# Unread products at the start of a scan, another order of the last weight loads, and row weights turned by a small product, in a state space block with a routed mixture of experts

## The reference

```python
xc = conv(in_proj_w @ ctx); u = silu(xc + conv_b)
dt_lo, Bm, Cm = split(x_proj_w @ u)
delta = softplus(dt_proj_w @ dt_lo + dt_proj_b)
# over the 256 positions, for each channel and each of 16 states:
state = state * exp(delta * A) + (delta * u) * B ; y = sum_n(state * C)
x = x + tanh(g_xattn) * (y + D * u) * silu(layernorm(x))
t = layernorm(x)
logits = t @ gate_w ; top 2 of 8 ; top_w = softmax(top two logits)
x = x + tanh(g_ffn) * sum_e top_w[e] * ((silu(t @ w0[e]) * (t @ w1[e])) @ wo[e])
```

## Time and profile before

| | |
|---|---|
| three runs | 294.03, 294.96, 295.08 us; median 294.96 |
| the profiled execution | 295.31 us, its span 293.1 us |
| busy share of the span | PE 89%, DVE 79%, ACT 63%, POOL 60% |
| mean granted clock of TensorE | 0.975 of full |
| chain that ended last | PE 60%, DVE 15%, issue 11%, POOL 6% |

### The profile page before, as it was taken

One profiled execution on the slowest core, in us unless ns is written; L12 is line 12 of the kernel. 1 busy time (PEld: TensorE's weight loads), 2 busy tenths in 40 slices (PEclk: granted clock), 3 DMA queues, 4 the chain that ended last, 5 costly groups with the idle time before them and its releaser, 6 DMA issues.

```text
span 293.1 us, 4667 instructions
## 1 busy us (share of the span) xinstructions
PE 261.4 (89%) x1177; PEld 177.8 (61%) x1178; DVE 231.1 (79%) x403; ACT 184.9 (63%) x343; POOL 175.1 (60%) x159
## 2 busy tenths in 40 slices
PE   7985597899888998888997999999999999999970
PEld 7432242344344354433476877989898989898960
DVE  2989979999999998999979649888565666566640
ACT  2895747865775657788895326565757575757540
POOL 6103168898999898989810331546564746464342
PEclk9999789999999999999999979999999999999996
DMA  7699400000000001000099310333333333333212
GB/s 237 201 390 386 178 2 0 1 0 0 0 1 2 1 0 72 0 0 3 0 330 356 122 54 22 47 61 46 63 48 62 48 62 48 59 50 57 32 25 36
DMA packets 16677, 22.73 MB, mean 78 GB/s; under 512 B 2570, under 2 KB 10290, under 8 KB 16658
## 3 DMA queue, kind: packets, MB, share of 16 engines
q1 hardware_dynamic: 11472, 16.41, 16.1%
q0 software_dynamic: 4416, 6.03, 12.6%
q10 hardware_dynamic: 770, 0.06, 0.2%
HBM read 17.38 MB, written 5.11 MB: 77 GB/s over the span
## 4 chain that ended last, share of the span: by engine, by line
PE 60%; DVE 15%; issue 11%; POOL 6%; ACT 3%; DMA 2%; POOLq 1%; DVEq 0%; ACTq 0%
PE PD L1062 11%; PE PZ L1102 11%; PE PU L1062 10%; PE PY L862 8%; DVE states L1270 5%; POOL hC L422 4%; PE PY L1088 4%; DVE states L1276 4%; PE PY L857 2%; PE PZ L1053 2%; PE PU L770 1%; PE PD L807 1%; PE PU L841 1%; DMA x_rows<-u 1%; PE PZ L903 1%
## 5 line engine op out<-in xcount | busy, mean ns | idle before, releaser
L422 POOL TENSOR_TENSOR hC<-states,WO 128x512 f32<-128x512 f32 x63 | 79.8, 1280 | 16.8 <-PE PY L862 11.7
L1276 DVE TENSOR_TENSOR_SCAN states<-PD,states 128x512 f32<-128x512 f32 x64 | 77.4, 1211 | 1.1 <-ACT PD L632 0.9
L862 PE MATMUL PY<-hC,ident 128*128 128x512 f32 x128 | 68.1, 616 | 4.1 <-POOL hC L422 3.8
L457 POOL DMA_INDIRECT out<-lg,y_at x23 | 37.0, 1607 | 48.3 <-ACT lg L736 41.1
L632 ACT ACTIVATE PD<-WO,Aneg 128x510 f32<-128x510 f32 x64 | 43.8, 688 | 16.9 <-DVE states L1276 13.7
L1270 DVE TENSOR_TENSOR states<-PU,WO 128x512 f32<-128x512 f32 x64 | 42.7, 669 | 2.6 <-POOL hC L422 1.3
L443 POOL DMA_INDIRECT hC<-x_rows,x_at x23 | 27.2, 1183 | 28.4 <-DMA x_rows<-u 17.3
L720 ACT ACTIVATE hidT_hi<-PY 128x512 fp32r<-128x512 f32 x23 | 13.8, 599 | 38.8 <-PE PY L1088 38.8
L1521 DVE TENSOR_TENSOR WO_lo<-WO,WO_hi 128x512 fp32r<-128x512 f32 x46 | 29.7, 687 | 6.1 <-issue 5.7
L862 PEld LDWEIGHTS PY<-hC,ident 128*128 128x128 f32 x128 | 22.7, 192 | 17.4 <-POOL hC L422 11.0
L1509 DVE TENSOR_TENSOR dA<-PU,dA 128x512 f32<-128x512 f32 x23 | 15.9, 690 | 21.1 <-PE PU L1062 21.1
(11 more groups left out here) (242 smaller groups left out, 505.6 us busy)
## 6 DMA issues: line engine op xcount, KB each, us to landing
W<-in_L_ffn_w SPq DMA_DIRECT2D x16, 512.0 KB, 10.5
WO<-in_L_ffn_wo SPq DMA_DIRECT2D x8, 512.0 KB, 6.4
xs<-in_x SPq DMA_DIRECT2D x2, 512.0 KB, 5.6
out<-xs SPq DMA_DIRECT2D x2, 512.0 KB, 4.9
early<-in_ctx SPq DMA_DIRECT2D x1, 512.0 KB, 4.3
x_rows<-u SPq DMA_DIRECT2D x1, 512.0 KB, 3.3
x_rows<-u SPq DMA_DIRECT2D x2, 256.0 KB, 3.1
hC<-x_rows,x_at POOLq DMA_INDIRECT x23, 3.2
```

Source lines behind the costliest of these rows:

```text
L422: pool.tensor_tensor(hC[:, n % 2, :], states[:, n % RING, :], C_rep[:, pair % C_RING, :], ALU.mult).then_inc(hc_done, 1)
L457: pool.indirect_dma_start(out=out, out_offset=bass.IndirectOffsetOnAxis(ap=y_at[:, s:s + 1], axis=0), in_=y_tile[s % 2], in_offset=None, c ...
L862: pe.matmul(PY[:, h, :], ident[:, :], hC[:, n % 2, :], start=False, stop=(m == DS - 1)).then_inc(y_done, 1)
L1276: dve.tensor_tensor_scan(states[:, n % RING, :], DEC[n % 2], states[:, n % RING, :], 0.0, ALU.mult, ALU.add).then_inc(scan_done, 1)
```

## The change

1. **Unread products at the scan's start.** Two products of the identity by `u`, 128x512, are put before `spread_B(0)` (into the bank that it then fills) and two before `spread_C(1)` (into bank 5). Nobody reads them.
2. **Rows and loads.** `normed` of the first 512 rows leaves tiles 59 to 62 and stands on ACT behind the last gates of the scan, ahead of the table load. SP loads wo of experts 0 to 3 first, then stores the three parts of `x_rows` and the second half of x2, and loads wo of experts 4 to 7 last. Each pair of experts has a semaphore of its own, and ACT waits for a pair only at the first slot that can use it.
3. **Row weights.** In the second run of one-hot products the operands are exchanged, so that the result lies as 48 x 128 (`W_ROWS`); ACT copies it, and one small product with a doubled identity (`two_id`, made by POOL at the start) turns it back and adds the two parts. DVE copies once where it copied and added. The layout of `slot_w` is changed to suit.
4. **Fills.** "placed" 8 to 4, "rows" (three times 1) gone, "weights" 6 to 7, "turned" 4 (new, behind the row weights); "turn" stays 3. `xT_out(0, 0)` on ACT moves ahead of `WO_out(0, 0)`.

```diff
-NORMED_AT = (59, 60, 61, 62)
...
-FILL = {"placing": 10, "placed": 8, "rows": 1, "weights": 6, "table": 1, "turn": 3}
+FILL = {"placing": 10, "placed": 4, "weights": 7, "table": 1, "turned": 4, "turn": 3}
...
+        W_ROWS = bank[4][0:2 * COLS, 0:P]
...
             store_x2(0)
             sp.wait_ge(dbu_done, NT)
             sp.wait_ge(exp_done, NT)
-            store_rows(0)
             load_WO(0)
             load_WO(1)
+            store_rows(0)
+            store_x2(1)
+            store_pair(2)
+            store_pair(3)
+            sp.wait_ge(x2_ps, NQ * QB)
+            load_WO(2)
             sp.wait_ge(hc_done, NT - 1)
             sp.wait_ge(last_hc, 1)
             load_WO(3)
-            sp.wait_ge(x2_ps, NQ * QB)
-            load_WO(2)
-            store_x2(1)
-            store_pair(2)
-            store_pair(3)
...
-                    if n in NORMED_AT:
-                        normed((NORMED_AT.index(n),))
...
             base_out(1)
+            normed(range(QBLK))
             act.preload_act_table_set("natural_log_exp_and_others")
...
-            act.wait_ge(ld["wo"], 16 * E)
...
+            act.wait_ge(w_rows_ps, 1)
+            act.activation(w_rows[:, :], W_ROWS, ACT.Copy).then_inc(w_rows_ok, 1)
+            xT_out(0, 0)
             act.wait_ge(slots_ok, 1)
+            act.wait_ge(WO_in[0], 32)
             WO_out(0, 0)
-            xT_out(0, 0)
             xT_out(1, 1)
...
             for s in range(4):
+                if s % 2:
+                    act.wait_ge(WO_in[(s + 1) // 2], 32)
                 expert_tile(s, s % 2, 16 * ((s - 1) // 2) if s > 2 else None)
+            act.wait_ge(WO_in[3], 32)
...
+            pe.wait_ge(taps_ok[1, 0], DC - 1)
+            for _ in range(2):
+                pe.matmul(BCR[0], ident[:, :], u[:, 0, 0, :], start=True, stop=True)
             pe.wait_ge(sel_ok, 1)
             pe.wait_ge(consts, 7)
             spread_B(0)
...
             x_dbl(1)
+            for _ in range(2):
+                pe.matmul(PY[:, 1, :], ident[:, :], u[:, 0, 0, :], start=True, stop=True)
             spread_C(1)
...
             for j in range(n):
                 if j % 4 == 0:
-                    if j:
-                        fill("rows", PD[1][:, :])
                     pe.wait_ge(row_hot_ok, j // 4 + 1)
...
-                mm = pe.matmul(bank[5][:, 0:2 * COLS].rearrange("p (i s) -> p i s", i=2), row_hot[:, j, :], slot_w[:, :, j, :], start=(j == 0), stop=(j == n - 1))
-            mm.then_inc(w_at_ps, 1)
+                mm = pe.matmul(W_ROWS, slot_w[:, j, :, :].rearrange("p i s -> p (i s)"), row_hot[:, j, :], start=(j == 0), stop=(j == n - 1))
+            mm.then_inc(w_rows_ps, 1)
+            fill("turned", PD[1][:, :])
...
             x_turn(0, 0, 16)
+            pe.wait_ge(two_ok, 1)
+            pe.wait_ge(w_rows_ok, 1)
+            pe.matmul(bank[5][:, 0:COLS], w_rows[:, :], two_id[:, :], start=True, stop=True).then_inc(w_at_ps, 1)
             fill("turn", PD[1][:, :])
...
             dve.tensor_copy(w_at[:, :], bank[5][:, 0:COLS]).then_inc(w_at_ok, 1)
-            dve.wait_ge(w_at_ok, 1)
-            dve.tensor_tensor(w_at[:, :], w_at[:, :], bank[5][:, COLS:2 * COLS], ALU.add).then_inc(w_at_ok, 1)
```

25 lines of the change are left out of this document (15 added, 10 removed).

## The result

| | before | after |
|---|---|---|
| median of four runs | 294.54 us | 297.28 us (296.14 to 298.51) |
| profiled execution | 295.31 us, span 293.1 | 296.14 us, span 294.2 |
| granted clock in it | 0.975 | 0.989 |

A forecast was written before the change was run, and what follows sets the result against it. The scan was taken as DVE-bound with POOL close behind, then latencies, then PE's products. Terms summed to -2.97 us, 0.3 was given back: 292.6 for the profiled execution, 292.3 against the median, range 291.2 to 294.8.

The forecast's parts named there:

- Scan, -2.05: Scan's start: unread products keep PE's clock up, so DVE's three idle stretches go, saving 2.05 us.
- rival 1: Scan's start: the clock still falls, only later; DVE keeps some 1.3 of 2.05 us, 293.6 us; chance 0.18.
- Norms, +0.5: Behind the scan: the moved norms delay ACT's copy; DVE waits and everything behind is late by 0.5 us.
- table and row weights: Between scan and slot 0: exchanged products and changed fills bring PE to the turn at the old time, 0 us.
- Rival 3: Table: one clock fall of some 3.4 us makes PE 0.7 to 1.4 late, about 293.3 us; chance 0.15.
- rival 4: Table to gate: the clock fall lasts 6.8 us, costing PE 4.5 us; slower, 296 to 297.5 us; chance 0.08.
- Gather, +0.4: First gather: shares the DMA engines in halves with the last loads, 0.4 us longer; ends 0 and +2.7.
- rival 2: First gathers: loads hold gather 0 for 1.5 to 2.7 us, delaying all slots, 293.4 to 294.6 us; chance 0.12.
- Store, -0.5: Last store: finds an empty queue instead of 4 MB of wo, saving 0.5 us; bounds 0 and -1.0.
- Second hole, -0.35 and -0.97: Just before and in slot 0: PE stays at 2.4 GHz, saving 0.35 us on fills and 0.97 on the gate.

The follow-up runs named there:

- e12: e3 with the norms of the first rows at their new place behind the scan: 296.91 us, ratio 1.012.
- e3: The changed kernel with part 2 undone (SP's old order, norms at tiles 59 to 62): 293.94 us, ratio 1.001.
- e11: The changed kernel with the loads of experts 4 to 7 held until gathers 0 to 3 have landed: 296.20 us, ratio 1.008.
- e2: The changed kernel with the loads of experts 4 to 7 held until gathers 0 and 1 have landed: 299.72 us, ratio 1.021.
- f5: e12 with the fills of the kernel before: 297.87 us, ratio 1.012.
- f6: e12 with fourteen "placing" fills instead of ten, ahead of PE's idle stretch: 294.65 us, ratio 1.003.
- e6: The changed kernel with only the loads of experts 6 and 7 held until gathers 0 to 3 have landed: 296.18 us, ratio 1.007.
- e10: Kernel before with parts 1 and 3, five more unread products, three fills behind the row weights, loads of experts 4 to 7 held for four gathers: 292.86 us.
- f1: e11 with the fills of the kernel before: 294.75 us, ratio 1.004.

## Why the prediction was wrong

**Scan, -2.05: right in the profile, wrong in the median.** All three idle stretches of DVE went and the scan ended 1.8 us earlier. But a profile is one execution. Over 12 runs part 1 alone brings 0.2 us, for two reasons. The clock falls near 34 us in part of the executions all the same (nine of 14 profiles), so rival 1 was a matter of how often, not whether. And the loss that was to be won back is not in every execution of the kernel before: two of four profiles without the products have a scan that ends just as early. The argument against rival 1, that no fall had followed the gap ahead of 23.96, rested on one execution too: in three of those four the clock falls at 24.2 to 25.2, right behind that gap. The sum took the clock of one execution, and a long one, for that of all.

**Norms, +0.5: the failed step.** The direct cost was right, even too high (0.3 us from scan to slots). What failed is that the step ended there: the place of the norms costs 3 us in the median (e12 against e3), by the clock. It said "everything behind that is late by 0.5", but not that PE idles for the same time ahead of "placed" (1.60 to 1.89), while part 4 took fills away behind it, for which the sum had no price: "table and row weights" was put at 0 with the clock up. Rival 3 looked at that stretch, but with the clock falling for 3.4 us and beside a gain of the scan; rival 4 had the length, 6.8 us, and the result, 296 to 297.5 (the change 297.28, e12 296.91), and I gave it 0.08. A fall of 6.8 us or more is in the profiles of e12, e11, e2 and f5, with the idle stretch at 1.9 us, and f6 shows that filling the stretch undoes most of the loss. It is in that of e3 too, with 1.60, so the new place is not the only way to it; in the one trace of the change itself the fall lasted 3.4 us, and that its three longer executions had a longer one is inferred from their clocks.

**Gather, +0.4: mis-sized, +3.24 measured.** It was worked out from sharing the engines by halves; the gather moved its first packet 2.5 us later than with empty engines, and landed at 169.48. The upper end, +2.7, was still too low by 0.5. This is rival 2; its 293.4 to 294.6 assumed the scan's gain in every run. On PE it costs 2 us where the clock falls for 3.4 us only (the change against e6 and f6).

For the halves I had leaned on the Trainium skill ("DMA: Bandwidth & Descriptors", "Issuing engines are not separate DMA queues"), by which DMAs of both issuers share the same 16 engines and interleave. This trace is in line with that: from 167 to 168 both queues move packets, and their shares are 100.3% and 13.0% of the 16 engines' time. The same page ("Queues, rings and completion order") says that each engine goes round the queues for which it has work, a packet's worth at a time; by that the gather should have moved its first packet about as soon as with empty engines. With 1 MB of loads ahead it did (1.9 us in e6, 2.2 before). With 2 MB ahead the first packet comes only after 4.4 to 4.7 us, and the gathers of four kernels land after 6.1 to 6.4 us against 2.9 to 3.3 with empty queues. The measurement decides. What holds the gather, the engines or something ahead of them, no run here shows.

**Store, -0.5:** -1.3 measured (3.44 to 2.12), below the bound of -1.0.

**Table and row weights, 0:** with the clock up, four groups of exchanged products with their fills take 1.8 us (164.83 to 166.63), nearly the 2.1 taken; "turned" takes 1.14 at 2.4 GHz, where 0.94 was taken. But the seven fills "weights" took 3.28 us at 1.2 GHz where the six of before took 1.63, which only the late gather hid.

**Second hole, -0.35 and -0.97:** measured -0.05 and -0.98 in the profile. The fills came down by 0.36, but the small product took 0.33 and not 0.2, on top of fills of 0.90 and not 0.70. And this hole too was one draw: of the six profiles with the old norms and fills only that of before has it.

The two failures don't add up. The late gather and the fallen clock delay the same event, the turn of slot 0, and the later of them sets it: 6.47 us behind the gather's issue for the loads (after), 4.65 to 5.24 for the clock (e12, e11), 3.2 with neither. So mending the loads alone (e11) gives back 1 us of 2.7 to 3.4, and restoring the loads' order alone (e12) nothing. Mending both (e3, f6) leaves 0.3% or less.

**The chances.** Faster had 0.62, resting on one profile's clock for the scan and on a clock that stays up behind it. Two conditions that vary from run to run belong in the sum with their frequency, and there the signs were against the change: a gain in few runs (part 1), a loss in nearly all (part 2). That the result fell into rival 4's range owes something to luck, since that range had the scan's gain in it as well.

## What to carry to other kernels

Before a small transfer that the chain waits for, count the bytes already queued on the DMA engines by anyone and price it as landing at their end, or after its own latency if that is later, not as having a share. Here 1 MB of loads ahead cost the gather 0.4 us, and 2 MB cost it 3. Bulk that is issued right behind the small transfer can hold it as well (6.3 us in e10), so hold bulk back until the small ones that follow soon have landed too, not only the first. When an edit delays an engine off PE's path, look at how long PE now idles and what clock it has afterwards: an edit that delays the path by 0.3 us cost 1.5 to 3 us in the median here, and four unread products in the idle stretch gave 1.0 to 2.3 back. And a fall of the clock seen in one profile is one draw, the kernel before's included: before giving its removal a gain, profile or time the old kernel often enough to know in how many executions the fall is there.

## What the runs showed of the hardware

- A gather of 128 KB issued by POOL right behind 2 MB of loads issued by SP lands after 6.08 to 6.42 us, its first packet 4.4 to 4.7 us behind the issue (1.9 to 2.2 with empty engines); behind 1 MB it lands after 3.6, and issued 0.3 us ahead of 2 MB after 6.3. A store of 256 KB behind 4 MB on SP's own queue lands after 8.53. On empty queues they take 2.9 to 3.3 and 2.0 to 2.1.
- The clock falls at different places where the work is the same: at 24.2, 25.0, 25.2 and 32.5 us in four profiles whose PE work is the same up to the scan's end. The kernel before, over 124 runs, had mean clocks of 0.972 to 0.991 and times of 291.7 to 296.7; the spread is larger than the effect of any part of the change but part 2.
- The falls to 1.2 GHz lasted 3.4 us (the kernel after, f1, f6), 6.8 (the first hole of before, e12, e3) or 10.2 (f5, e2), and went on through stretches in which PE was busy all the time. They began up to 3.3 us behind the end of the idle stretch: 0.2 in f1, 1.1 in e12, 3.3 in the kernel after.
